# Three kinds of transposes moved from TensorE to the DMA queue in a Mamba and feed-forward layer

## The reference, cut to what matters

```
x  = x + layernorm(attn(layernorm(x)));  x = x + layernorm(ffn(layernorm(x)))
attn: xi = x @ Wx.T; z = x @ Wz.T; xs = silu(causal_conv4(xi) + conv_b)      # 512 features, 8 heads of 64
      b = xs @ Wb.T; c = xs @ Wc.T; dt = softplus(xs @ Wdt.T + b_dt)          # dt: one step size per head
      state = exp(dt*a) * state + dt * b (outer) xs;  y = c . state           # scan over 1024 steps
      y = y + d*xs;  per-head norm over time and head;  out = (yn * silu(z)) @ Wout.T
ffn:  gelu(x @ bin(w1).T + b1) @ bin(w2).T + b2                               # hidden 1024, bin = alpha*sign
```

## Time and profile before

| | |
|---|---|
| median of 3 runs | 1320.47 us (1318.77 to 1324.37) |
| the profiled execution | 1318.21 us, its span 1316.5 us |
| TensorE busy | 1255.9 us, 95% |
| VectorE busy | 985.4 us, 75% |
| ScalarE busy | 850.5 us, 65% |
| GpSimd busy | 480.2 us, 36% |
| DMA, mean busy share of 16 engines | 7.3% for the queue of the loads and stores |

### The profile page before, as it was taken

How to read it: one execution, slowest core, us unless ns; L and a number is a source line. 1 busy time by engine, 2 the same in 40 slices (tenths; PEclk the granted TensorE clock), 3 DMA queues, 4 the chain that set the end, 5 groups by cost and what they waited for, 6 DMA issues and landing times.

```text
span 1316.5 us, 28386 instructions
## 1 busy us (share of the span) xinstructions
PE 1255.9 (95%) x10764; PEld 801.6 (61%) x10764; DVE 985.4 (75%) x2392; ACT 850.5 (65%) x1487; POOL 480.2 (36%) x575
## 2 busy tenths in 40 slices
PE   6998999999999999999999999999999999999675
PEld 4564657566575756656575665757566565756543
DVE  6575876878778686877868787786968778695674
ACT  6554676658765586765866677655867658565543
POOL 2031335143442534334342334514343253431533
PEclk9999999999999999999999999999999999999888
DMA  7010000101010010101001010000101000010100
GB/s 229 1 50 1 18 1 2 49 1 49 1 49 1 1 49 1 50 1 49 2 2 49 2 49 1 20 31 2 49 1 49 1 19 16 1 34 1 33 1 32
DMA packets 30568, 32.93 MB, mean 25 GB/s; under 512 B 1857, under 2 KB 28629, under 8 KB 30433
## 3 DMA queue, kind: packets, MB, share of 16 engines
q1 hardware_dynamic: 30432, 31.11, 7.3%
HBM read 22.72 MB, written 8.39 MB: 24 GB/s over the span
## 4 chain that ended last, share of the span: by engine, by line
PE 48%; DVE 34%; issue 7%; ACT 5%; POOL 5%; DVEq 0%; POOLq 0%; ACTq 0%
PE bank L1506 12%; PE bank L1705 8%; PE bank L1692 8%; DVE xs L1143 7%; PE bank L1597 4%; PE bank L1619 4%; DVE sh L1148 2%; DVE yT L1272 2%; PE bank L1589 2%; DVE hh L1322 2%; ACT un L911 2%; DVE gn_stats L1279 2%; DVE un L1119 2%; PE bank L1517 2%; PE bank L1642 2%
## 5 line engine op out<-in xcount | busy, mean ns | idle before, releaser
L1506 PE MATMUL bank<-sh,WbT 128*128 128x512 f16 x768 | 174.2, 383 | 4.6 <-DVE sh L1148 3.8
L1506 PE MATMUL bank<-sh,WcT 128*128 128x512 f16 x768 | 175.9, 379 | 0.0
L1143 DVE SCALAR_TENSOR_TENSOR xs<-xi,vectors,xs 128x512 f32<-128x512 f32 x168 | 128.4, 769 | 5.8 <-ACT xs L959 2.1
L831 POOL TENSOR_TENSOR Cd<-Cd,CT 128x512 f32<-128x512 f32 x64 | 81.4, 1272 | 135.6 <-ACT Cd L1054 135.5
L1506 PEld LDWEIGHTS bank<-sh,WbT 128*128 128x128 f16 x768 | 74.2, 98 | 91.0 <-DVE sh L1148 4.8
L1506 PEld LDWEIGHTS bank<-sh,WcT 128*128 128x128 f16 x768 | 75.2, 98 | 86.5
L1692 PE MATMUL bank<-uh,sign1T 128*128 128x512 f16 x512 | 121.8, 383 | 1.7 <-DVE uh L1345 1.7
L1705 PE MATMUL bank<-sign2T,hh 128*128 128x256 f16 x1024 | 120.0, 277 | 1.8 <-DVE hh L1358 1.8
L1083 ACT ACTIVATE hf<-bank,vectors,alpha 128x512 f32<-128x512 f32 x128 | 99.1, 777 | 33.4 <-PE bank L1692 26.1
L1705 PEld LDWEIGHTS bank<-sign2T,hh 128*128 128x128 f16 x1024 | 101.3, 99 | 15.7 <-DVE hh L1358 2.6
L1256 DVE TENSOR_TENSOR mt<-bank,mt 128x512 f32<-128x512 f32 x128 | 82.4, 685 | 36.1 <-PE bank L1619 36.1
(11 more groups left out here) (213 smaller groups left out, 2762.0 us busy)
## 6 DMA issues: line engine op xcount, KB each, us to landing
xt<-L_attn_input_tensor_dram SPq DMA_DIRECT2D x16, 512.0 KB, 5.0
u<-L_attn_input_tensor_dram SPq DMA_DIRECT2D x16, 512.0 KB, 4.0
out_dram<-u SPq DMA_DIRECT2D x16, 512.0 KB, 2.9
yT<-in_L_ffn_w_dram SPq DMA_DIRECT2D x2, 512.0 KB, 10.6
u<-in_L_ffn_w_dram SPq DMA_DIRECT2D x2, 512.0 KB, 8.4
BT<-in_L_attn_Wx_dram SPq DMA_DIRECT2D x1, 512.0 KB, 4.9
BT<-in_L_attn_Wz_dram SPq DMA_DIRECT2D x1, 512.0 KB, 4.2
zs<-in_L_attn_Wb_dram SPq DMA_DIRECT2D x1, 512.0 KB, 5.6
```

Of the source, the lines that this page charges most:

```text
L831: pool.tensor_tensor(Cd[n % 2][:, :, :], Cd[n % 2][:, :, :], CT[:, :, q * P:(q + 1) * P], ALU.mult)\
L1143: nc.vector.scalar_tensor_tensor(out=conv_sum(j, c), in0=xi[:, c, k:k + BLK], scalar=taps[:, c, k:k + 1], in1=conv_sum(j, c), op0=ALU.mult ...
L1506: mm = nc.tensor.matmul(bank(t, key)[:, :], w[i][:, k, cols(m)], v[h][:, k, :], start=(a == 0), stop=(a == len(terms) - 1))
```

## The change

It has four parts.

1. **Normed rows.** `xT` and `uT` are no longer TensorE steps, but for the first block (`first_turn`) and the last batch's feed-forward (`uP`). ScalarE writes the normed rows a first time in f16 (`turn[0]`), then in f32; VectorE subtracts to get the low half of the rows (`turn[1]`, one instruction of 1,024 elements); SyncE issues two DMA transposes into `xh` or `uh`. `turn` and `x_turned` lie in the tile `xi`, between the convolution's uses of it.
2. **The convolved input.** X is no longer turned on TensorE. SyncE issues, for each chunk, a DMA transpose of each half of `sh` into `x_turned`; VectorE adds the halves, then multiplies by the step sizes in place.
3. **Step sizes.** The two halves of `Wdt` lie side by side; a matmul of 16 columns and one of 8 take the place of three of 8 (32 in place of 48 a block). VectorE adds the two parts with one more row.
4. **Order.** All eight `H` stand behind the four C products, where they were between them; the input's statistics come before the first `H` on VectorE, and the input's norm behind the first `carry`.

The steps in `turn_steps`, for the middle of a block:

```diff
-        steps += own(("log", j))
+        steps += own(("X", j, 0), ("X", j, 1), ("log", j))
@@
-        steps += own(("C", j, 0), ("cums", j)) + tail(("uT", j)) + own(("roles", j), ("skip", j), ("C", j, 1))
-        steps += tail(("H", j, 0), ("H", j, 1)) + [(who, "in_stat", nj)]
+        steps += own(("C", j, 0)) + tail(("uT", j)) + own(("cums", j), ("roles", j), ("skip", j), ("C", j, 1))
-        steps += own(("C", j, 2)) + tail(("H", j, 2), ("H", j, 3)) + (own(("head_stat", 0, 0)) if j else [])
+        steps += own(("C", j, 2)) + [(who, "in_stat", nj)] + (own(("head_stat", 0, 0)) if j else [])
-        steps += own(("sums", j)) + tail(("H", j, 6), ("H", j, 7))
+        steps += own(("sums", j)) + tail(*[("H", j, f) for f in range(2, KF)])
@@
+        steps += own(("X", j, 2), ("score", j, 1), ("X", j, 3), ("carry", j, 0)) + norm + tail(("O", j, 1)) + own(("back", j, 0)) + xT
+        steps += own(("ends", j, 2), ("front", j, 2), ("score", j, 2), ("carry", j, 1), ("back", j, 1)) + tail(("end_stat", j))
+        steps += own(("ends", j, 3), ("front", j, 3)) + tail(("end_root", j)) + own(("score", j, 3))
```

The SyncE queue (new), the rows of ScalarE and VectorE (new), and the rows of the chunk:

```diff
+            def turn_input(t, j):
+                p, pj = before_block(t, j)
+                sp.wait_ge(*full(p, ("z", pj, KI - 1)))
+                sp.wait_ge(*xn_hi.count(t, (j + 1) * NQ))
+                sp.dma_start_transpose(turned_out(xh[0]), turn[0][:, :, :, :].rearrange("p k q d -> p (k q d)")).then_inc(xh_hi.sem, 16)
+                sp.wait_ge(*xn_lo.count(t, j + 1))
+                sp.dma_start_transpose(turned_out(xh[1]), turn[1][:, :, :, :].rearrange("p k q d -> p (k q d)")).then_inc(xh_lo.sem, 16)
...
+            def turn_tokens(t, j, q):
...
+                sp.wait_ge(*x_sum.count(s, ch(sj, sq) + 1))
+                for i in range(2):
+                    sp.dma_start_transpose(x_turned[r][:, i, :, :], sh_rows[i][:, q, :, :].rearrange("p c t -> p (c t)")).then_inc(x_rows[r].sem, 16)
@@
             def ff_norm(t, j):
+                if not after_last_input(t):
...
+                    for i in range(NQ):
+                        normal_high("ff", un_hi, u[j], t, j, i)
                 for i in range(NQ):
                     normal("ff", un, u[j], t, j, i)
@@
+                nc.vector.tensor_tensor(turn[1][:, :, :, :], by_feature(un[:, :, :]), turn[0][:, :, :, :], ALU.subtract)\
+                    .then_inc(un_lo.sem, 1)
@@
-                nc.vector.tensor_tensor(xdt[r][:, :, :], heads(bank(t, ("X", j, q))[:, :]), per_head(dt_t[:, q, :]),
-                                        ALU.mult).then_inc(xdt_out.sem, 1)
+                dve.wait_ge(*x_rows[q % 2].count(t, n // 2 + 1))
+                hi, lo = [x_turned[q % 2][:, i, :, :].rearrange("p c f -> p (c f)") for i in range(2)]
+                nc.vector.tensor_tensor(xdt[r][:, :, :], heads(hi), heads(lo), ALU.add).then_inc(x_sum.sem, 1)
+                dve.wait_ge(*x_sum.count(t, n + 1))
+                nc.vector.scalar_tensor_tensor(out=xdt[r][:, :, :], in0=xdt[r][:, :, :], scalar=1.0 / SX, in1=per_head(dt_t[:, q, :]),
+                                               op0=ALU.mult, op1=ALU.mult).then_inc(xdt_out.sem, 1)
@@
             def hidden(t, j, f):
                 key = ("H", j, f)
-                for need in latest(empty(t, key), uh_lo.count(t, (j + 1) * KD)):
-                    pe.wait_ge(*need)
+                if f == 0:
+                    pe.wait_ge(*uh_hi.count(t, j + 1))
+                    pe.wait_ge(*uh_lo.count(t, j + 1))
+                pe.wait_ge(*empty(t, key))
```

More of the change, by code:

```diff
@@ L417, in uses @@
                 return [("St", *at), *[("Y", *at, p) for p in range(HP)]]
[L418 to L419 removed]
+            if kind == "uP":
+                return [("uP", *at, k) for k in range(KD)]
             return [("gn",)] if kind == "gn_mean" else []
@@ new lines, in load_next, with load_middle, weights @@
+            def load_next(t, j):
+                if t.number() + 1 < NB:
+                    load_x(t.ago(-1), j)
+            def load_middle(t, j):
+                if t.number():
+                    load_u(t, j)
+            def weights(t, name, k):
+                if name == "ready":
+                    sp.wait_ge(act_set, ACT_SETUP)
+                    sp.wait_ge(dve_set, DVE_SETUP)
+                    for j in range(NJ):
+                        load_u(Batch(0), j)
+            all_batches(sp, {"first_turn": first_turn, "weights": weights, "xT": turn_input, "uT": turn_middle, "X": turn_tokens,
+                             "load": load_next, "load_u": load_middle, "end_add": store})
@@ L1333, in middle_norm @@
                 s, sj = before_block(t, j)
-                dve.wait_ge(*full(s, ("uT", sj, KD - 1)))
+                if after_last_input(s):
+                    dve.wait_ge(*full(s, ("uP", sj, KD - 1)))
+                else:
+                    dve.wait_ge(*un_lo.count(s, sj + 1))
                 for i in range(NQ):
```

294 lines of the change are left out of this document (175 added, 119 removed).

## The result

The change made the kernel slower: 1345.51 us median (1345.04 to 1347.16, four runs) beside 1319.62 us for the kernel before (1318.13 to 1324.37, four runs); the ratio is 1.0191, 95% interval 1.0175 to 1.0206. I had forecast 1284 us. The profiled execution of after has a span of 1345.4 us.

A forecast was written before the change was run, and what follows sets the result against it. TensorE's and VectorE's queues, the later at each place, were taken to bound it. Seven blocks at 2.5 us, seven at 2.0, 5 us for the first batch and 0 for the last tail made 36.5 us: 1284 us, range 1250 to 1340.

The forecast's parts named there:

- step 6: Chunks behind the second output product, VectorE leading: end at 689.2 us instead of 691.9, a gain of 2.7 us.
- the other kind of block: Block with the head's statistics in the chain ahead of the first `hh`: a gain of 2.0 us, chosen.
- Steps 1 and 2: Four C products end at 654.0 us; the low half ends at 650.4, the last `hh` at 665.2, late as before.
- The price of a DMA transpose: One turn of 256 KB taken as 3.5 us, hidden with 0.9 us to spare in the model block.
- The rivals of late and slow turns: Turns somewhat late (third rival): 1288 to 1320 us, chance 0.22; bound by their own rate: 1348 or 1450, chance 0.18.
- Step 4: Feed-forward products paced by VectorE's `hh` rows: the first output product ends at 667.5 us, 0.8 us earlier.
- Step 5: Up to the end of the second output product: 8.2 us instead of 9.5, end at 675.7, 2.1 us earlier.
- the sum of halves takes over 1 us: Sign of being wrong: VectorE's addition of the halves for each chunk, priced at 0.69 us, exceeds 1 us.
- Step 7: Convolution after the chunks: VectorE is full, so 2.7 us are carried on; step sizes take 0.2 back, leaving 2.5.
- TensorE 87 us less busy: Sign in the profile after: 20 + 20 + 40 us of transposes and 7 us of step-size products leave TensorE.
- VectorE 45 us more: Sign in the profile after: VectorE busier by 64 times 0.7 and step sizes, less the shorter low halves.
- The granted clock in TensorE's new pauses: Sign of being wrong: the granted clock falls when TensorE pauses where it did not before; no size given.

The follow-up runs named there:

- root_late_alone: The kernel after with only GpSimd's end root moved from in front of the third state scaling to behind it: 1344.3 us, ratio 1.0178.
- the cut kernel: The kernel after with GpSimd's product `Cd` cut to 8 of 128 columns a head pair: 1331.84 us, ratio 1.008.

## Why the prediction was wrong

**What the parts are worth**, read along one path by ratios: order +2.0% (26 us), norm rows by DMA from there -2.1% (27 us, from 1.0197 to 0.9989; the step sizes and the input norm's new place are in this), the convolved input by DMA +2.0% (27 us). The parts do not simply add. With the old end order the norm rows are worth only -1.1% (1.0064 to 0.9951) and the convolved input costs +2.7% (0.9951 to 1.0225). I had forecast a gain without costing the order as a part of its own.

**The step that failed** is step 6, the chunks behind the second output product: VectorE's new rows were priced as if GpSimd did nothing beside them, and the root that moved with the end statistics was not followed into GpSimd's queue. With it failed the 2.0 us for the other kind of block, a term that was chosen and not followed through the queues.

- *Steps 1 and 2* held. First `hh` 13.1 us after the first C product (forecast 12.9). The low half ended 7.7 us after it (forecast 6.8), and the roles and `hh` rows behind it took 14.0 us (forecast 14.8), so the last `hh` ended within 0.2 us of the forecast. Part of the lateness is a stretch that I had not priced: this low half took 1.51 us beside GpSimd's `yT` rows, and 1.23 in the other kind of block, where GpSimd is idle.
- *The price of a DMA transpose*: taken 3.5 us, measured 3.1 for the norm rows and 2.5 for the convolved input. The first hidden product started right behind the last C product, with 0.2 us idle. The rivals of late and slow turns, on which I had put all of the chance of "slower", did not happen. The Trainium skill, VectorE: DVE Perf Modes, in The three transpose paths, would have given an estimated 10.5 us for eight tiles in a row; no turn here took that, the longest took 4.5 us.
- *Step 4* (0.8 us earlier at O0) was 0.4. Nearly right, as VectorE's queue was followed there. But the table shows it as a difference of larger terms: the order loses 0.7 us in this stretch (24.64 to 25.34), the norm rows win back 0.6 (24.71), the convolved input 0.5 (24.25).
- *Step 5* (8.2 us to O1) was 9.03. With X on TensorE this stretch takes 9.02 as well, so the X group that I counted as gone bought nothing here; TensorE waited 0.50 us for `mt` instead.
- *Step 6 failed, and decides in this block.* It gave 13.5 us from O1 to b3 (675.7 to 689.2), and the trace has 17.2. Two terms. The rows: low half 1.25 and sum 0.69 were 1.75 and 1.76 in chunk 2, and `xdt` of chunk 3 was complete 11.9 us behind O1 where I had 10.2. I priced them by nearest rows that ran without a GpSimd row beside them. The sign I had written down, "the sum of halves takes over 1 us", came true (1050 ns). Then "TensorE's last three groups (2.3 us)" behind `xdw`: they took 4.2, from 701.29 to 705.47. I had counted the moved end statistics on VectorE, but did not follow the root, moved with them, into GpSimd's queue, where it now stands ahead of the state's scaling. Of these 1.9 us the root is 1.3, by root_late_alone (4.70 to 3.45); the rest is that TensorE's product with the state waits for the scaling and VectorE's row, where I had three groups back to back. The two terms, 1.7 and 1.9 us, turn the forecast gain of 2.7 us at b3 into a loss. The root's 1.3 us is not won by moving it alone, as that run shows.
- *The other kind of block* was given 2.0 us of gain by choice. It lost 1.6 us in the mean, and the model block lost 2.6 where I had a gain of 2.5. Seven of each make 61 us, which is the whole difference between 1284 and 1345.5. The first batch gained 1.6 us (forecast 5); the last tail, put at 0, belongs to a stretch that grew by 2.5.
- *Step 7* (what is won in chunks is carried on) holds in its reverse: b3 to C stayed at 27.2, so the loss was carried on in full.
- *TensorE 87 us less busy*: 41. The 87 us are the busy times of groups that overlap their neighbours. Counted from each product's start to the next one's, the rows that went had filled 71.8 us, and the products that stayed fill 30.5 us more, 7.7 of them the hidden products. *VectorE 45 us more*: 71. The two `xdt` rows take 120.0 us where one took 44.1; against the lengths of the cut kernel, 1050 for 703 and 826 for 691 ns, 64 times each, 31 us of that are stretch.
- *The granted clock in TensorE's new pauses* had been named as a sign of being wrong. It came true four times (half clock for 3.4 us each) and cost 1 or 2 us in all at most.
- *In the rivals' sums* the lower bound of the third should read 1291, not 1288 (1284 + 7).

The mutual stretch could have been known in advance. The trace of the kernel before has it, where the convolution's `xs` row meets GpSimd's sum `u`:

```profile
691.81 4.13 POOL L799 TENSOR_TENSOR u<-u,y 128x256 f32<-128x256 f32 x4
...
695.28 2.78 DVE L1143 SCALAR_TENSOR_TENSOR xs<-xi,vectors,xs 128x512 f32<-128x512 f32 x3
```

The first of these three `xs` rows takes 1.21 us and the others 0.75, and the four `u` rows take 4.13 us where each takes 0.72 alone. The price 0.77 us for `xs`, which I used for the product, is a mean that hides seven such meetings. The rule also stands in the Trainium skill, SBUF — State Buffer, in SBUF: two separate sides: VectorE and GpSimd share one port pair as an exclusive lock, and a VectorE instruction with two SBUF inputs takes it against a GpSimd one that reads SBUF; the other blocks for its whole length. The trace agrees: low half, `Cd` and sum take 1.23, 1.27 and 0.68 us alone, and behind the end of `y` at 690.37 they ended one after the other, at 691.45, 692.58 and 693.13, so 1.08, 1.13 and 0.55 us apart. That is a little less than their lone lengths, so they are not fully serial. In the kernel before `xdt` read a bank and one SBUF operand and took 0.69 us beside `Cd`, and `Cd` kept its 1272 ns. By this rule the low half and the sum of chunk 2 should have been priced with a collision, 1.6 us a block.

What stays open: the stretch was priced (at most 14 us by the cut of `Cd`, of which 2 show without the change) but not removed in a version that keeps everything. The other 13 us of the convolved input's part are the added row itself, the packets and what they push on; they were not parted further. Nor was the input norm's new place tried by itself.

## What to carry to other kernels

A transpose that leaves TensorE for the DMA queue is only as cheap as the rows that it leaves behind: the norm rows, whose halves ScalarE and one VectorE row prepare beside other work, gained 1 to 2%; the convolved input, whose two halves had to be added in each chunk, lost 2 to 3%, though both turned in some 3 us. When an operand moves from PSUM to SBUF, look at what GpSimd does at that moment, and price the VectorE row as its own length plus what is left of GpSimd's. When steps move in a common order, print the moved place for every engine, the least busy one too: GpSimd was busy 36% of the time, and on the kernel before the end order, which puts a 1.2 us step in front of its state row, cost 18 us. Follow each kind of block, too: the one that I did not follow made two fifths of the miss.
